# Second layer of a four-layer graph network: value projection in three float32r passes, adjacency tiles sent for at another point, constants loaded after the first tiles

## The reference, cut to what matters

```python
# layer 1
H_  = jnp.einsum('nd,hde->hne', H, W)
out = jnp.einsum('nm,hme->hne', adj, H_) + b[:, None, :]
x   = _layernorm(x + out)
# layer 2, what is prepared from this x
values = h @ fc_w + fc_b
s1 = (h @ W[:IN_C]) @ a_w        # kept as two extra columns beside fc_w,
s2 = (h @ W[IN_C:]) @ a_w        # (u2 = W @ a_w, folded once)
e  = jnp.where(adj > 0, e, NEG_BIG)   # rows of adj turned into a mask, row by row
```

## Time and profile before

| what | us |
|---|---|
| median of 3 runs | 3456.7 (3454.18 to 3467.5) |
| the profiled execution | 3455.23 |
| its span in the trace | 3453.4 |
| the adjacency stage: last barrier to next barrier, about | 1110 to 1601 |
| first adjacency matmul | 1126.54 |
| transposes of the first and of the last normed tile (L138) | 1151.85 and 1583.08 |

### The profile page before, as it was taken

The page is one execution under the profiler, slowest core; times in us unless marked ns, Lnnn a source line. Parts: engine busy times, 40 slices in busy tenths (PEclk is TensorE's granted clock), DMA queues, the critical chain, the costliest instruction groups (busy, mean ns, idle before and its releaser), DMA issues. The chain is left out here.

```text
span 3453.4 us, 38132 instructions
## 1 busy us (share of the span) xinstructions
PE 3077.8 (89%) x14683; PEld 2184.4 (63%) x14683; DVE 2604.7 (75%) x3257; ACT 1953.4 (57%) x1740; POOL 255.4 (7%) x441
## 2 busy tenths in 40 slices
PE   5799999999977999994999986999999966999994
PEld 4533333333333777773888865888888725898993
DVE  5599999999955566665777746888888655788877
ACT  0299999999932221112444427888888414566652
POOL 0000000000011111111000010000101000000003
PEclk9999999999999999997999997999999988999997
DMA  7600000000023576667333328676767522888884
GB/s 274 235 15 11 17 9 16 16 16 8 8 73 119 203 267 256 246 245 272 136 128 107 127 70 319 240 278 242 279 245 271 206 89 75 297 295 290 290 286 156
DMA packets 143059, 581.08 MB, mean 168 GB/s; under 512 B 16016, under 2 KB 30067, under 8 KB 124704
## 3 DMA queue, kind: packets, MB, share of 16 engines
q1 hardware_dynamic: 120288, 443.45, 35.7%
q0 software_dynamic: 22592, 135.19, 10.9%
HBM read 374.87 MB, written 203.71 MB: 168 GB/s over the span
## 5 line engine op out<-in xcount | busy, mean ns | idle before, releaser
L516 PE MATMUL bank<-dist,hf 128*65 128x512 f32 (+2 forms) x2112 | 805.1, 543 | 12.3 <-ACT dist L478 12.3
L516 PEld LDWEIGHTS bank<-dist,hf 128*65 128x65 f32 x2112 | 290.5, 138 | 518.9 <-issue 484.0
L1387 PE MATMUL bank<-pt,HA 128*128 128x256 f32 x1936 | 505.7, 381 | 4.5 <-DMA HA<-features 4.5
L478 ACT ACTIVATE dist<-dist 128x1408 f32<-128x1408 f32 (+1 forms) x352 | 452.9, 1322 | 4.6
L1656 DVE TENSOR_TENSOR w<-w,whi 128x1280 fp32r<-128x1280 f32 (+1 forms) x176 | 282.6, 1619 | 93.0 <-ACT whi L1616 92.2
L1314 DVE COPY pt<-bank 128x512 f32<-128x512 f32 (+1 forms) x440 | 264.3, 630 | 113.3 <-PE bank L1375 111.5
L1387 PEld LDWEIGHTS bank<-pt,HA 128*128 128x128 f32 x1936 | 328.9, 191 | 28.2 <-DMA HA<-features 4.7
L1616 ACT ACTIVATE whi<-w 128x1280 fp32r<-128x1280 f32 (+1 forms) x176 | 242.8, 1380 | 181.0 <-DMA w<-weights 178.8
L409 DVE TENSOR_TENSOR dist<-msk,sB 128x1408 f32<-128x1408 uint8 (+1 forms) x208 | 324.8, 1562 | 23.4 <-PE bank L516 13.9
L1375 PE MATMUL bank<-idt,v 128*128 128x128 f32 x1936 | 302.0, 276 | 41.6 <-ACT v L1261 33.6
L469 ACT ACTIVATE dist<-dist,neg_t 128x1408 f32<-128x1408 f32 (+1 forms) x208 | 295.1, 1419 | 60.1 <-DVE dist L409 56.8
(11 more groups left out here) (168 smaller groups left out, 5104.8 us busy)
## 6 DMA issues: line engine op xcount, KB each, us to landing
weights<-pt SPq DMA_DIRECT2D x220, 512.0 KB, 3.8
w<-weights SPq DMA_DIRECT2D x88, 768.0 KB, 6.9
w<-weights SPq DMA_DIRECT2D x88, 640.0 KB, 5.5
al<-in_adj_cols SPq DMA_DIRECT2D x22, 1408.0 KB, 8.3
at<-in_adj_tiles SPq DMA_DIRECT2D x22, 1408.0 KB, 7.9
rows<-in_adj_rows SPq DMA_DIRECT2D x22, 1408.0 KB, 6.8
HB<-in_adj_rows POOLq DMA_DIRECT2D x22, 1354.0 KB, 7.6
rows_low<-HB POOLq DMA_DIRECT2D x22, 1354.0 KB, 5.9
```

The costliest lines, as they stand in the source:

```text
L478: act.activation(d[:, 0:VALID[c]], d[:, 0:VALID[c]], ACT.Exp, scale=-1.0).then_inc(p_ready, 1)
L516: mm = pe.matmul(sums_bank(hh, k)[0:FW, 0:hi - a * P], hf[hh][:, m, :], d[:, a * P:hi], start=(m == 0), stop=(m == T - 1))
L1387: t = pe.matmul(acc_t[n % 2][:, 0:P2], HA[:, m, h * D3:(h + 1) * D3], pt[n % 2][:, m, :, :].rearrange("p r n -> p (r n)"), start=(m == 0), ...
```

## The change

Four things are done, all in the adjacency stage.

1. The projection behind block 17 is made of three float32r passes instead of one float32 product. ACT's copy of the turned tile is now the high part `xth`; a new DVE instruction (`turned_low`) subtracts it from the PSUM bank and gives the low part `xtl`; `fc_w` with its two score columns is split once into `wh` (ACT) and `wl` (DVE). PE issues 24 matmuls in a tile.
2. SP sends for `at[q]` of tile `j` when `lo_ready` shows that both halves of tile `j-2` have been split, no longer when its matmuls are done.
3. The constants are loaded behind the first two `at` loads. PE no longer waits for them at its start; DVE waits for them behind its first three `lo` halves.
4. `bias`, `vb`, `xin`, `R` and the raw `w_sb` lie in `HB` and no longer in buffers of their own.

```diff
@@ SP
-                    sp.dma_start(bias[:, :], b1.partition_broadcast(P)).then_inc(c_in, 16)
-                    sp.dma_start(w_sb[:, :, 0:D // 2], fc_w[:, :, 0:D // 2]).then_inc(c_in, 16)
...
                             j = 2 * i + q
-                            wait(sp, half_done, 2 * (j - 1))
+                            wait(sp, lo_ready, 2 * (j - 1))
                             sp.dma_start(at[q][:, :, :], adj_tiles[j]).then_inc(at_in[q], 16)
+                            if j == 1:
+                                sp.dma_start(bias, b1.partition_broadcast(P)).then_inc(c_in, 16)
+                                sp.dma_start(w_sb[:, :, 0:D // 2], fc_w[:, :, 0:D // 2]).then_inc(c_in, 16)
+                                sp.dma_start(w_sb[:, :, D // 2 + 2:D + 2], fc_w[:, :, D // 2:D]).then_inc(c_in, 16)
+                                sp.dma_start(vb, fc_b.partition_broadcast(P)).then_inc(c_in, 16)
                             wait(sp, r_full, T + j - 1)
@@ PE
-                    pe.wait_ge(c_in, 64)
...
                             pe.wait_ge(ln_done, T + j + 1)
+                            wait(pe, xl_ready, j)
                             turn_tile(pe, n, xn[q])
...
-                        project(pe, n, xt[q], w_sb, (D // 2 + 2, D // 2))
+                    def values(n, j, q):
+                        if j == 0:
+                            pe.wait_ge(w_ready, 3)
+                        pe.wait_ge(xl_ready, j + 1)
+                        wait(pe, proj_out, n)
+                        for into, a, b in ((pj, 0, D // 2 + 2), (sc, D // 2 + 2, D + 2)):
+                            for k in range(KT):
+                                pe.matmul(into[0:P, 0:b - a], xth[q][:, k, :], wh[:, k, a:b], start=(k == 0), stop=False)
+                                pe.matmul(into[0:P, 0:b - a], xth[q][:, k, :], wl[:, k, a:b], start=False, stop=False)
+                                t = pe.matmul(into[0:P, 0:b - a], xtl[q][:, k, :], wh[:, k, a:b], start=False,
+                                              stop=(k == KT - 1))
+                        t.then_inc(proj_mm, 1)
@@ DVE
-                    dve.wait_ge(c_in, 64)
-                    dve.tensor_copy(w_sb[:, :, D // 2:D // 2 + 2], u2[:, :, :]).then_inc(w_ready, 1)
+                    def turned_low(j):
+                        q = j % 2
+                        dve.wait_ge(turned_out, 2 * T + j + 1)
+                        dve.tensor_tensor(xtl[q][:, :, :], etp_view(), xth[q][:, :, :].bitcast(FP32), ALU.subtract)\
+                           .then_inc(xl_ready, 1)
...
                     rest(1, 1, 0)
+                    dve.wait_ge(c_in, 64)
+                    dve.tensor_copy(w_sb[:, :, D // 2:D // 2 + 2], u2[:, :, :]).then_inc(w_ready, 1)
+                    dve.wait_ge(w_ready, 2)
+                    dve.tensor_tensor(wl[:, :, :], w_sb, wh[:, :, :].bitcast(FP32), ALU.subtract).then_inc(w_ready, 1)
...
                                 rest(j + 1, 1 - q, 1)
+                            turned_low(j)
@@ ACT
                     rounded(1, 0, 1, 0)
+                    act.wait_ge(w_ready, 1)
+                    act.activation(wh[:, :, :], w_sb, ACT.Copy).then_inc(w_ready, 1)
...
-                            keep_turned(act, 2 * T + j, xt[q])
+                            keep_turned(act, 2 * T + j, xth[q])
```

More of the change, by code:

```diff
@@ L624, in build @@
         with ExitStack() as ph:
-            R, xn, st, xin, xt, bias, w_sb = norm_buffers(ph, (128, KT, D + 2))
+            space = HB[:, :, :].rearrange("p t d -> p (t d)")
+            bias, vb = (space[:, (10 + k) * D:(11 + k) * D] for k in (0, 1))
+            xin, R = ([space[:, (12 + 2 * k + q) * D:(13 + 2 * k + q) * D] for q in (0, 1)] for k in (0, 1))
+            w_sb = space[:, 16 * D:16 * D + KT * (D + 2)].rearrange("p (k c) -> p k c", k=KT)
+            xn = [sb(ph, f"xn{q}", [P, D]) for q in (0, 1)]
+            st = [sb(ph, f"st{q}", [P, 10]) for q in (0, 1)]
+            xth, xtl = ([sb(ph, f"{n_}{q}", [128, KT, P], F32R) for q in (0, 1)] for n_ in ("xth", "xtl"))
+            wh, wl = (sb(ph, n_, [128, KT, D + 2], F32R) for n_ in ("wh", "wl"))
             at = [sb(ph, f"at{q}", [P, T, P]) for q in (0, 1)]
@@ L628, in build @@
             lo = [sb(ph, f"lo{half}", [P, HT, P], F32R) for half in (0, 1)]
-            vb = sb(ph, "vb", [P, D])
             srow = sb(ph, "srow", [T, P])
-            space = HB[:, :, :].rearrange("p t d -> p (t d)")
             mrow, low = space[:, 0:N], space[:, N:N + N // 4]
@@ L634, in build @@
             vh, vl = ([sb(ph, f"{n_}{q}", [P, D], F32R) for q in (0, 1)] for n_ in ("vh", "vl"))
-            vt_ready, vh_ready, vl_ready, v_stored = sem("vt_ready"), sem("vh_ready"), sem("vl_ready"), sems("v_stored")
+            xl_ready, vh_ready, vl_ready, v_stored = sem("xl_ready"), sem("vh_ready"), sem("vl_ready"), sems("v_stored")
             mrow_in, low_ready, mrow_ready, mrow_stored = (sem(k) for k in ("mrow_in", "low_ready", "mrow_ready", "mrow_stored"))
@@ L646, in _ @@
                 def _(sp):
-                    sp.dma_start(bias[:, :], b1.partition_broadcast(P)).then_inc(c_in, 16)
-                    sp.dma_start(w_sb[:, :, 0:D // 2], fc_w[:, :, 0:D // 2]).then_inc(c_in, 16)
-                    sp.dma_start(w_sb[:, :, D // 2 + 2:D + 2], fc_w[:, :, D // 2:D]).then_inc(c_in, 16)
-                    sp.dma_start(vb[:, :], fc_b.partition_broadcast(P)).then_inc(c_in, 16)
                     def body(i):
@@ L668, in tail @@
                             pe.wait_ge(ln_done, T + j + 1)
+                            wait(pe, xl_ready, j)
                             turn_tile(pe, n, xn[q])
                         else:
[L671 to L675, removed]
-                        project(pe, n, xt[q], w_sb, (D // 2 + 2, D // 2))
+                            values(n, j, q)
+                    def values(n, j, q):
[10 more added lines that the diff above has]
+                        t.then_inc(proj_mm, 1)
                     def body(i):
@@ L710, in v_out @@
                         wait(dve, vl_ready, j - 1)
-                        dve.tensor_tensor(vt[q][:, 0:D // 2], pj[0:P, 0:D // 2], vb[:, 0:D // 2], ALU.add).then_inc(vt_ready, 1)
+                        dve.tensor_tensor(vt[q][:, 0:D // 2], pj[0:P, 0:D // 2], vb[:, 0:D // 2], ALU.add).then_inc(part_out, 1)
                         dve.tensor_scalar(f2[0:P, 0, bass.ds(j, 1)], pj[0:P, D // 2:D // 2 + 1], ab2[0:P, :], None, ALU.add)\
```

## The result

| | us |
|---|---|
| predicted | 3421 (3407 to 3442) |
| changed kernel, median of 4 runs | 3421.36 (3418.22 to 3424.71) |
| kernel before, 4 runs beside it | 3455.44 (3452.71 to 3467.5) |
| ratio | 0.9895, 95% interval 0.9869 to 0.9921 |
| profiled execution, its span | 3419.75, 3417.9 |

The change makes the kernel faster by 1.05% (0.79 to 1.31), and the time forecast is met. The span is shorter by 35.5 us. What follows compares the changed kernel ("after") with the rows of before, and each term with its measured size, since a sum can be right with wrong terms.

The account below looks back on a forecast made before the run. The load-mask-store ring was taken to bound the adjacency stage, PE close behind. Turns of 19.1 instead of 20.60 us give 30, the start 5: 3455.2 less 35 is 3420.2, plus 1.5 for the median, said as 3421 (3407 to 3442).

Parts of the forecast that it names:

- What bounds the kernel: Adjacency stage: two close limits, PE's 19.30 us a tile and the load-mask-store ring; what ends last is mostly the ring.
- The ring: Adjacency row load, mask, store, next load through one buffer and POOL's queue: 19.70 us usual, 20.60 mean, 18.67 forecast.
- Part 1, `at`: Sending `at` earlier, off the mask row's store: store 6.51 to 5.20 us, -1.3 a turn; load to mask 7.4.
- The allowance of 0.4 for scatter: Added to the adjacency turn because landings scatter and two limits lie close: 19.1 us.
- Part 2, the product: Projection in three float32r passes: 3.63 to 3.04 us, -0.59 a tile, PE's work 18.71.
- Part 3, the new instructions: `turned_low` (0.69 us) fits DVE's 1.40 pause; splitting weights, 2.4 us once on DVE, taken as 0.
- Part 4, the start: Stage start, first `at` ahead of the constants: gain 5 us, between 2.5 and 8.7.
- The sum: Turn 19.1 against 20.60 gives 30 us over 20 turns, start 5: 35 less, forecast 3421.
- The first: Rival: `at` overlaps the row load's end, making it 8.4 us, turn 19.7 to 20; 3434 to 3440; chance 0.17.
- The second: Rival: the mask row's store isn't slow because of `at`; ring stays 20.6, only start counts; 3448 to 3454; chance 0.09.
- third: Slower rival: `at` hits every row load, load to mask 10.06 us, turn 21.33; 3466; chance 0.05.
- fourth: Slower rival: weight loads aren't hidden in the projection, 7.4 us, PE 23.1 a tile; about 3500; chance 0.02.

Follow-up runs that it names:

- e5: Changed kernel plus a second adjacency-row buffer, so the next row loads before the mask row's store is waited for: 3402.04 us, 0.9836 of before.
- e6: e5 with `at` sent for at the old point, when the matmuls are done: 3402.02 us, 0.9835 of before.
- e10: Kernel before plus only the second row buffer (float32 product, old `at` point, constants first): 3422.71 us, 0.9910 of before.
- e11: Changed kernel with `xin` of a tile sent for only behind the next tile's `at`: 3420.54 us, 0.9903 of before.
- e1: Changed kernel with `at` sent for at the old point, when the matmuls are done: 3457.76 us, 1.0007 of before.
- e2: Changed kernel with the float32 product back in place of the three passes: 3421.26 us, 0.9890 of before.
- e4: Kernel before plus the three float32r passes, with the new buffer places and waits for constants: 3470.24 us, 1.0026 of before.
- e8: Changed kernel with POOL's power for the next tile ahead of the wait for the mask row's store: 3418.52 us, 0.9882 of before.
- e9: Kernel before plus the new `at` point, with the new buffer places and waits for constants: 3428.66 us, 0.9926 of before.
- e3: Changed kernel with the four constant loads moved in front of SP's loop again: 3428.41 us, 0.9910 of before.

## Why the prediction was right, point by point

**What bounds the kernel: right.** The ring was read from POOL's wait and from three intervals. e5, e6 and e10 show it by opening it: the turn falls to PE's own, and POOL's wait stops mattering.

**Part 1, `at`: right in the step, and in half of its account.** `at` was put 4.3 us behind the row load, and it is 4.36; load to mask was put at 7.4, and it is 7.26. The store was put at 5.20, as the one without other traffic; the usual one takes 5.54, since `xin` is issued 3.3 us behind it (e11: 5.2 without). The quiet ring is 18.87, not 18.67. The allowance of 0.4 for scatter had no row behind its size; it measures 19.28 - 18.87 = 0.41. Of this, three stores of 7.3 to 7.5 us make 3 x 1.9 / 20 = 0.28 (see the last section). The turn came out at 19.28 for 19.1, so the turns gave 26.3 us and not 30. POOL's wait fell to 110.4 us where about 100 was named as the sign.

The prediction gave the whole gain of a turn to the store (-1.3) and put the row load's at nothing ("there is little to gain and 7.36 may stay"). The means say -0.71 for the store and -0.61 for the way from row load to mask. The 7.36 was the reading of one quiet tile; the mean of before was 8.02, since `at` at its old point also lay on the row load in many turns (the earlier trace rows shows the worst). The term came into the sum unnoticed, because a quiet ring of after was set against a mean turn of before. That the size nearly fits is luck here; that moving `at` is the cause is shown by e1.

**Part 2, the product: too small in length, wrong in worth.** The passes start 0.12 us apart, as in the earlier trace rows:

```profile
1187.92 0.28 PE L684 MATMUL bank<-wh,xth 128*128 128x258 f32 x1
1188.04 0.28 PE L685 MATMUL bank<-wl,xth 128*128 128x258 f32 x1
1188.16 0.28 PE L686 MATMUL bank<-wh,xtl 128*128 128x258 f32 x1
```

PE's own turn was put at 18.71 and is 18.44 (e5), against 19.24 before (e10): the saving is 0.80 us, not 0.59. The 18.69 between two transposes of after meets the 18.71 only because it holds a pause of 0.25. From the first instruction of the product to the next adjacency matmul it is 3.28 us in the tile of the earlier trace rows (1157.88 to 1161.16) and 2.85 in after (1150.47 to 1153.32), where the prediction took 3.63 and 3.04, both with the tail of the last instruction, behind which the next has already begun; and the adjacency matmul behind the float32 product took 0.43 us to the next one instead of 0.24. The rest of the 0.80 was not traced. The rule quoted from the Trainium skill ("TensorE: Matmul & The Clock Gate", section "Part 3: Packing small matmuls — row/col tiling") would have made it 23.1; the measurement decides against it here, for full-height float32r passes with other weights each time. But the sum took the larger of ring 18.67 and PE 18.71, and so let the shorter product count: without it the same sum would have said 19.30 plus the allowance. e2 measures a turn of 19.24 without it and the same time. Two limits that lie so close don't add their scatter as I had it: with 19.24 of PE work in a turn, most of the ring's bad turns are hidden.

And one sentence was too mild: that a faster product alone "would be given back as a longer wait at L138". The wait does come (46.4 us in e4 against 24.7), but it is more than given back (e4, +0.26%), most likely since PE's end is also what sends `at` off. The prediction named each of these facts and didn't join them.

**Part 3, the new instructions: right.** `turned_low` stands in the pause, with 0.79 left of 1.40. The split of the weights is hidden in the wait for the first tiles; DVE's row:

```profile
1135.45 2.30 DVE L759 TENSOR_TENSOR wl<-HB,wh 128x2056 fp32r<-128x2056 f32 x1 [1.99 <-ACT wh L819]
```

It was put at 2.4 us, and PE comes to the first transposes without a wait 9 us later, at 1144.51.

**Part 4, the start: right in mechanism, sized too low.** 7.85 us against 5 (and 2.5 to 8.7 as ends). The middle was taken for want of a row on how much the first row load and the second `at` would slow the first `at`. They slow it little: ACT begins at 1117.59, 6.7 us behind the issue, near the shortest landing and far from the 12 of before.

**The sum** met the time because errors cancel: -30 was -26.3, -5 was -7.85, and the rest, put at nothing, gave 1.3. That 3421 meets 3421.36 so closely is luck; the terms are off by up to 4 us each.

**The rivals.** The first (the row load takes what the store gives) doesn't occur in after: load to mask is 7.41 in the mean, 8.0 to 8.3 in three turns, and DVE waits 3.6 us in all. Its mechanism exists, and sets e8. The second (the store isn't slow because of `at`) falls with e1 and e9, but for the 0.3 us that `xin` does cost the usual store (e11). The third and fourth would have shown a load of 10 and a product of 7.4 us; neither is there.

## What to carry to other kernels

Look for a buffer that is loaded, changed and stored in one in-order queue that other work passes through: its turn is the sum of two landings and the work between, and a second buffer takes it away as a whole: here it gave 0.90% alone, about as much as the four parts of the change together, and with them 1.64%. Where one transfer is moved off another, read the means of all steps of the ring over many turns, and not one quiet turn: the second transfer that it had slowed gave nearly half of the gain. A transfer whose issue hangs on a compute engine's progress moves when that engine gets quicker, so read what it will fall on. And a term that shortens an engine which isn't the limit should stand in the sum with zero, and its worth be read again once the ring is open: here 0 before and 11 us after.

## What the runs showed of the hardware

**Of these two large transfers, the one issued first is largely served first.** The store (1354 KB, POOL's queue), from its issue to the next load's, against the time at which `at` (1408 KB, SP's queue) was issued, in 57 turns of before, e1 and e4:

| `at` issued, against the store | turns | store us, median (range) |
|---|---|---|
| 0.63 ahead to 0.30 behind | 9 | 10.8 (9.7 to 11.2) |
| 0.58 to 0.85 behind | 10 | 6.6 (6.2 to 8.6) |
| 1.0 to 2.1 behind | 28 | 6.3 (5.95 to 7.9) |
| 2.4 to 3.6 behind | 10 | 5.9 (5.2 to 6.6) |

With no `at` near it the store takes 5.2. So a store of 5.2 us whose rival comes 0.6 us later is slowed by 1.4 only, and one whose rival comes half a microsecond earlier by 5.6. The queues show it directly. These are the transfers of e1's store of 1237.54 (q1 carries SP's, q0 POOL's), first from its issue to 1242.04, then from there to 1248.34:

```profile
q1 hardware_dynamic: 99, 1.12, 94.4%
```

```profile
q0 software_dynamic: 144, 1.39, 51.8%
q1 hardware_dynamic: 189, 0.59, 26.8%
```

For 4.5 us behind its issue not one packet of the store has moved; `at` has the engines. The other way round, in e4, with `at` issued 0.72 us behind the store of 1201.28, SP's queue has no packet up to 1206.28:

```profile
q0 software_dynamic: 128, 1.39, 82.2%
```

In the prediction I read the Trainium skill ("DMA: Bandwidth & Descriptors", section "Queues, rings and completion order") as going round between queues packet by packet, so that who comes first is not served first. These rows don't agree with that reading: with even sharing from 0.7 us on, the 4.5 us that a store of 5.2 has left would take some 9, and the store 9.7 (an estimate from these rows), where 6.6 is measured. The same section of the Trainium skill says that an engine drains a whole packet, which it puts at some 9 to 17 descriptors, before it turns to another queue. The trace counts 144 records (its "packets") for the store, 9 for each of 16 engines; if these are descriptors of one packet, the rule allows what is measured and only the conclusion from it was wrong. That, and which part of the path keeps the order, no run here shows.

**An instruction-fetch transfer inside a store goes with a slow store.** The transfers of two stores of after, by queue (packets, MB, share of 16 engines), first that of 1344.33 to 1351.75, then that of 1325.37 to 1331.02:

```profile
q0 software_dynamic: 144, 1.39, 46.4%
q1 hardware_dynamic: 144, 0.26, 10.8%
q8 instruction: 1, 0.02, 1.1%
```

```profile
q0 software_dynamic: 144, 1.39, 58.9%
q1 hardware_dynamic: 138, 0.25, 17.0%
```

The first took 7.42 us, the second 5.65, with the same bytes but for one packet of instructions. In the 105 stores of after, e2, e3, e9 and e11, 13 have such a packet and take 6.0 to 7.6 us (median some 7.0); the 92 without one have a median of 5.37, and the highest is 6.15. A longer store has more chance to hold such a packet, but that alone would leave some long stores without one, and none above 6.15 us is. That they go together is measured; that the packet is the cause was not tried.

**A wait of PE costs more than itself.** In e1 a wait of 7.29 us was followed by transposes of 1.11 us instead of 0.60 and matmuls of 0.63 instead of 0.39, at the lower of the clock's two levels, before it rose again at about 1254.2. Over 20 turns that came to 0.53 us a turn beside the waits. The prediction named the clock only in its lower bound.
